# Storing each tile of gathered embeddings in three parts, and loading its first unit in another order

## The reference: what is computed

```
e = stack([tbl_f[ids[:, f]] for f in range(24)], axis=1)      # 1024 x 24 x 16
Xk = X0 = e
for W in (W0, W1, W2):                                        # 64 outputs each
    Xk = einsum('bfd,bhd,fho->bod', X0, Xk, W)                # products of every field with every row of Xk
    outs.append(Xk.sum(axis=2))
h = concatenate(outs + [dense_ctx], axis=1)                   # 1024 x 208
y = relu(relu(h @ W_top1 + b1) @ W_top2 + b2) @ W_top3        # 1024 x 1
```

## Time and profile before

| what | value |
|---|---|
| median of three runs | 424.27 us (423.68 to 428.24) |
| profiled execution, its own time | 421.92 us |
| its span, from first to last instruction | 420.1 us |
| mean granted TensorE clock | 0.955 |
| TensorE busy | 342.1 us, 81% |
| VectorE busy | 288.5 us, 69% |
| ScalarE busy | 189.7 us, 45% |
| POOL busy | 233.2 us, 55% |
| DMA, moved | 73.63 MB, mean 175 GB/s |

### The profile page before, as it was taken

One profiled execution on the slowest core, in us unless ns is written; L12 is line 12 of the kernel. 1 busy time (PEld: TensorE's weight loads), 2 busy tenths in 40 slices (PEclk: granted clock), 3 DMA queues, 4 the chain that ended last, 5 costly groups with the idle time before them and its releaser, 6 DMA issues.

```text
span 420.1 us, 6106 instructions
## 1 busy us (share of the span) xinstructions
PE 342.1 (81%) x2296; PEld 150.5 (36%) x2296; DVE 288.5 (69%) x277; ACT 189.7 (45%) x346; POOL 233.2 (55%) x252
## 2 busy tenths in 40 slices
PE   0045899438396969599999997999999999999997
PEld 0043422102041323244333433543444344443466
DVE  2001499129385959578987998798899999898700
ACT  1000026113335345273737573757556475745374
POOL 5775888888888888788788887677400000000000
PEclk9998899859886999999999999999999999999999
DMA  3355936499799998999799979998999799731000
GB/s 101 74 111 116 231 83 157 83 231 234 164 242 233 252 257 152 228 231 213 163 228 223 232 137 222 233 235 163 225 251 266 156 251 258 214 107 44 2 2 2
DMA packets 59263, 73.63 MB, mean 175 GB/s; under 512 B 31489, under 2 KB 36609, under 8 KB 59234
## 3 DMA queue, kind: packets, MB, share of 16 engines
q1 hardware_dynamic: 53090, 71.66, 74.2%
q0 software_dynamic: 6144, 1.59, 3.2%
HBM read 48.05 MB, written 1.58 MB: 118 GB/s over the span
## 4 chain that ended last, share of the span: by engine, by line
PE 68%; DMA 10%; issue 9%; POOL 3%; another core or an unknown queue 2%; ACT 2%; SPq 2%; DVE 1%; DVEq 0%; ACTq 0%
PE ps_x L370 44%; PE ps_tower L370 9%; PE ps_turn L370 6%; PE ps_b L370 5%; POOL x_rows L191 3%; DMA A<-x_scratch 3%; DMA B_sb<-x_sb 2%; DMA x_scratch<-x_rows 2%; PE ps_turn L415 2%; PE ps_turn L423 1%; SPq L256 1%; DMA C<-x_scratch 1%; DVE Z L337 1%; PE ps_tower L376 1%
## 5 line engine op out<-in xcount | busy, mean ns | idle before, releaser
L347 DVE TENSOR_TENSOR Z<-A,ps_b 128x1024 f32<-128x1024 f32 x192 | 222.0, 1214 | 29.5 <-remote 18.8
L191 POOL DMA_INDIRECT x_rows<-tbl,ids_sb x192 | 190.8, 994 | 62.6 <-issue 43.6
L370 PE MATMUL ps_x<-Z,w_sb 128*64 128x512 f32 x768 | 188.4, 609 | 1.7 <-issue 1.0
L337 DVE TENSOR_TENSOR Z<-A,C 128x1024 f32<-128x1024 f32 x48 | 58.1, 1224 | 75.5 <-DMA C<-x_scratch 37.4
L370 PEld LDWEIGHTS ps_x<-Z,w_sb 128*64 128x64 f32 x768 | 50.3, 139 | 84.3 <-issue 65.8
L370 PE MATMUL ps_x<-Z,w0s_sb 128*64 128x512 f32 x192 | 48.3, 626 | 24.4 <-DVE Z L337 23.9
L635 ACT ACTIVATE x_diag<-ps_turn,mask_sb 128x192 f32<-128x192 f32 x128 | 50.6, 606 | 9.9 <-PE ps_turn L423 9.8
L618 ACT COPY ps_b<-B_sb 128x1024 f32<-128x1024 f32 x45 | 46.4, 1030 | 9.8 <-DMA B_sb<-x_sb 5.9
L648 ACT COPY G<-ps_turn 128x416 f32<-128x416 f32 x31 | 15.7, 506 | 73.5 <-remote 45.8
L599 ACT COPY x_sb<-ps_x 128x512 f32<-128x512 f32 x16 | 9.4, 586 | 78.2 <-PE ps_x L370 78.2
L204 POOL MEMSET pause_sb<- 128x768 f32 x56 | 42.3, 756 | 3.6 <-DMA x_scratch<-x_rows 3.6
(11 more groups left out here) (48 smaller groups left out, 147.2 us busy)
## 6 DMA issues: line engine op xcount, KB each, us to landing
A<-x_scratch SPq DMA_DIRECT2D x48, 512.0 KB
B_sb<-x_sb SPq DMA_DIRECT2D x90, 256.0 KB
C<-x_scratch SPq DMA_DIRECT2D x32, 512.0 KB
x_rows<-tbl,ids_sb POOLq DMA_INDIRECT x192
x_quarters<-x_scratch SPq DMA_DIRECT2D x16, 96.0 KB
x_scratch<-x_rows SPq DMA_DIRECT2D x7, 192.0 KB
w_sb<-w SPq DMA_DIRECT2D x2, 384.0 KB
C<-x_scratch SPq DMA_DIRECT2D x2, 256.0 KB
```

Source lines behind the costliest of these rows:

```text
L191: pool.indirect_dma_start(out=x0_rows[t % 2][:, f * D:(f + 1) * D], out_offset=None, in_=tables[f], in_offset=bass.IndirectOffsetOnAxis(ap ...
L337: nc.vector.tensor_tensor(Z[s % ZR][:, :], A[u % AS][i][:, :], C[u % 2][i][:, :], ALU.mult).then_inc(z_ready, 1)
L347: nc.vector.tensor_tensor(Z[s % ZR][:, :], A[u % AS][i][:, :], ps_b[j % 2][:, :], ALU.mult)\
L370: return nc.tensor.matmul(out, lhsT, rhs, start=start, stop=stop)
```

## The change

The store of every tile is cut into the three parts that tile 0 has. Part i waits for its own 8 gathers and has its own semaphore. SP issues parts 0 and 1 where it stored the whole tile. For the first (even) unit of a tile it then loads `A 0` (needs part 0), `C 0` and `A 1` (need parts 0 and 1), issues the store of part 2, waits for it, and loads `C 1` and `A 2`. For odd units the order becomes `C 0`, `A 0`, `C 1`, `A 1`, `A 2`. For tile 1, part 0 is stored ahead of the `B` loads of unit 1, and part 1 behind them. POOL waits for each part of the tile before last ahead of that part's gathers, in place of one wait for the whole.

```diff
-            def store_tile(t):
-                sp.wait_ge(gathered[t % 2], 16 * F * ((t + 1) // 2))
-                store_rows(t, slice(0, F), x0_stored[t % 2])
+            def store_part(t, i):
+                sp.wait_ge(part_gathered[t % 2][i], 16 * FR * (t // 2 + 1))
+                v = x0_dram[t:t + 1, FR * i:FR * (i + 1), :].rearrange("t f (b d) -> (t b) f d", d=D)
+                src = x0_rows[t % 2][:, D * FR * i:D * FR * (i + 1)].rearrange("p (f d) -> p f d", d=D)
+                sp.dma_start(v, src).then_inc(part_stored[t % 2][i], 16)
...
                 for f in range(F):
+                    if t >= 2 and f % FR == 0:
+                        wait_stored(pool, t - 2, f // FR)
...
                 if u == 2:
+                    store_part(1, 0)
                     for k in range(NJ - 1):
                         load_b(u - 1, k)
-                    store_tile(1)
-                if u % 2 == 0:
-                    wait_stored(sp, u // 2)
+                    store_part(1, 1)
                 sp.wait_ge(z_ready, made_x1(u - 2, NI - 1))
-                for i in range(NI - 1):
-                    load_c(u, i)
                 for i in range(NI):
+                    if u % 2 == 0 and i > 0:
+                        wait_stored(sp, u // 2, i)
+                    if u % 2 == 0 and i == 1:
+                        load_c(u, 0)
+                    if u % 2 == 0 and i == 2:
+                        load_c(u, 1)
+                    if u % 2 == 1 and i < NI - 1:
+                        load_c(u, i)
+                    if u % 2 == 0 and i == 0:
+                        wait_stored(sp, u // 2, 0)
                     if u >= AS:
                         sp.wait_ge(z_ready, made_x2(u - AS, NP2 - NI + i))
                     load_a(u, i)
+                    if u % 2 == 0 and i == 1:
+                        store_part(u // 2, 2)
...
                 if u % 2 == 1 and u + 1 < UNITS:
-                    store_tile((u + 1) // 2)
+                    for i in range(NI - 1):
+                        store_part((u + 1) // 2, i)
```

More of the change, by code:

```diff
@@ L128, in cin_tower @@
         ids_in = sem("ids_in")
[L129 to L132, removed]
+        part_gathered = [[sem(f"part_gathered{p}{i}") for i in range(NI)] for p in range(2)]
+        part_stored = [[sem(f"part_stored{p}{i}") for i in range(NI)] for p in range(2)]
         ident_in, mask_in, pick_in, w0_in, w1_in, tower_in = (sem(n) for n in (
@@ L175, in after, with wait_stored @@
                 engine.wait_ge(semaphore, count)
[L177 to L182, removed]
+        def wait_stored(engine, t, i):
+            engine.wait_ge(part_stored[t % 2][i], 16 * (t // 2 + 1))
         block = ctx.enter_context(nc.Block())
@@ L196, in _ @@
             for f in range(F):
-                gather(0, f, gathered_part[f // FR])
-            pool.wait_ge(part_stored[NI - 1], 16)
+                gather(0, f, part_gathered[0][f // FR])
+            wait_stored(pool, 0, NI - 1)
             for t in range(1, TILES):
-                if t >= 2:
-                    wait_stored(pool, t - 2)
                 for f in range(F):
+                    if t >= 2 and f % FR == 0:
+                        wait_stored(pool, t - 2, f // FR)
                     if f % BURST == 0:
@@ L207, in _ @@
                     after(pool, z_ready, PER_SLOT * (2 * t - 5) + 2 * PER_SLOT * f // F)
-                    gather(t, f, gathered[t % 2])
+                    gather(t, f, part_gathered[t % 2][f // FR])
         @block.sync
@@ L264, in _ @@
             for i in range(NI):
-                sp.wait_ge(gathered_part[i], 16 * FR)
-                store_rows(0, slice(FR * i, FR * (i + 1)), part_stored[i])
-                sp.wait_ge(part_stored[i], 16)
+                store_part(0, i)
+                wait_stored(sp, 0, i)
                 if i > 0:
@@ L560, in _ @@
             pe.wait_ge(ident_in, 16)
-            pe.wait_ge(part_stored[1], 16)
+            wait_stored(pe, 0, 1)
             keep_warm(WARM[0])
```

## The result

| | before | the change |
|---|---|---|
| median of 20 runs | 423.77 us (419.96 to 428.24) | 424.02 us (421.86 to 432.55) |
| ratio, 95% interval | 1 | 1.0073 (1.0039 to 1.0107) |
| profiled execution, its own time | 421.92 us | 425.59 us |
| its span | 420.1 us | 423.7 us |
| granted TensorE clock, mean | 0.955 | 0.944 |

The ratio leaves disturbed executions out, so it says more than the two medians. The change costs 0.7%, some 3 us, where a gain of 2.7 us was predicted. The two spans differ by 3.6 us.

A forecast was written before the change was run, and what follows sets the result against it. TensorE (busy 81% of the span) and a nearly full DMA queue were taken as bounds. A 6.7 us opening gain less five extra pauses of 0.8 us gave -2.7 us from 424.27: 421.5 us predicted, range 416.5 to 429.

The forecast's parts named there:

- d = 0.8: Later tiles: two DMA queue pauses per tile last 0.8 us longer together than today's one of 2.6 us.
- The pause behind part 2: Later tiles, before `C 1`: SP waits for part 2's store, queue dry some 2.0 us, at most 3.0.
- the pause before `A 0`: Later tiles: SP waits for part 0, partly filled by part 1's store and the quarters, leaving 0.9 to 1.9 us.
- the lower bound: Later tiles: both pauses sum to 2.9 us, an extra of 0.3 us per tile over today's one.
- the skewed rings: Later tiles' DMA queue: rings skewed by full loads lengthen a pause, so the extra was put above its smallest value; no separate size.
- The upper bound, 2.3: Later tiles: both pauses as long as today's, 4.9 us together, an extra of 2.3 us per tile.
- the sum it gave, +3.3: Whole kernel: a fixed 2.0 us per additional waited store in each tile gives -6.7 + 10, slower by 3.3 us.
- the opening's term: Unit 2: three loads moved into the nearly idle queue bring its `B` 6.7 us earlier; 6.5 us for the engines.
- part 2's store is issued at 75.1: Tile 1: SP issues this store when it issued the whole one, but behind `A 1`; it lands at about 80.4 us.
- -6.7 + 5d: TensorE's shift at unit 14: the opening's 6.7 us gain less five tiles' extra pauses, predicted -2.7 us.
- The rival of the double pause: Even units: the queue drains twice at full price, 2.3 us extra per tile, time 429.1 us; chance 0.2.
- My slack: ScalarE's copy of `C`: room before a later `C 1` delays it, 9.0 us at unit 6, 3.0 at 12, 1.2 at 14.

The follow-up runs named there:

- the opening alone: Against the kernel before, only tile 1 is stored in three parts with the new load order for unit 2; tiles 2 to 7 stay whole, old order: ratio 1.0038.

## Why the prediction was wrong

**The step that failed: d = 0.8, the extra pause of a later tile.** It is 2.2 to 2.3 us by the dry stretches (1.6 by the count over all of them) and 2.3 on average by the copies of slots 5 to 15. The pause behind part 2 was put at 2.0 to 3.0 us and is 2.5. What was mis-sized most is the other one: the pause before `A 0` was put at 0.9 to 1.9 us, because part 1's store and the quarters would fill it, and it is 2.4. They fill next to nothing. I chose d near the lower bound because the part stores are small. The size of the store hardly matters: the queue is dry for 2.4 and 2.5 us with stores of a third, for 2.6 with whole ones. No trace takes a pause apart into receipt, issue and first byte, and no run shows the skewed rings that the choice of d mentions. The upper bound, 2.3, is what was measured. The rule of the Trainium skill that was weighed (page "DMA: Bandwidth & Descriptors", section "Anatomy of one DMA — SWDGE (gpsimd) path", a fixed cost of about 2.0 us) was nearer than my choice; that section speaks of DMAs issued by GpSimd, while these stores are issued by SyncE, and the 2.2 to 2.3 us of the trace agree with it in size. That the sum it gave, +3.3, is close to the +3.6 of the spans is chance, since the opening's term was off.

**The opening: the mechanism held, its size was off.** The loads started about when predicted (`A 0` issued at 69.61, DMA share 0.92). The step that part 2's store is issued at 75.1 "as the whole store was" failed by 5.4 us, since the last gathers land 5.2 us after the end of POOL's instruction when the queue is full, not 1.3. Unit 2's `B` came 3.4 us earlier and not 6.7 (4.4 on the later chip). That the change then was 8.1 ahead in slot 5 of the first chip is not its merit by these steps.

**POOL was in the way at unit 4.** Part 2 of tile 2 was stored at 119.76, predicted about 120, but that agreement is luck. SP had issued `A 1` at 114.41 and then stood for 4.8 us, until the last gather of tile 2, which POOL had ended at 113.20, had landed:

```profile
114.41 0.60 SPq L226 DMA_DIRECT2D A<-x_scratch  x1
119.76 0.38 SPq L219 DMA_DIRECT2D x_scratch<-x_rows  x1
```

`C 1` was issued at 125.52, and ScalarE waited 9.6 us for it. A part of the lead went past tile 2's gathers (3.8 us in slot 4); with a wait for the whole tile POOL takes nearly all of it away.

**The sum.** The form -6.7 + 5d was sound as far as the trace tells. With what was measured in slot 5 and d = 2.3 it is -8.1 + 11.5 = +3.4, where the spans differ by 3.6. With d = 2.3 and the predicted opening it would have been +4.8, as the rival of the double pause said, and with the 3.4 us of unit 2's `B` +8.1. The rival of the double pause had d right. That the loss stayed at 3 to 4 us rests on the first chip's slot 5, which is luck.

**The slack at ScalarE's copy of `C`.** I expected tile 3 to pay nothing and unit 14 to wait. On the first chip it was the other way: units 6, 8 and 10 waited 9.7, 6.4 and 5.0 us. My slack took queue and engines to be early by the same amount. But at unit 6 the queue was 2.7 ahead (158.62 against 161.31), the engines 8.1 in slot 5, and at unit 10 `C 1` landed 7.5 later in its unit instead of 5.4. On the later chip every even unit waited, unit 6 for 8.9 us and also unit 14, for 7.6. So tile 3 pays on both chips, against the prediction, and the wait in unit 14 came on one of them.

**The clock was left out.** The prediction counts waits alone. In the later tiles the granted clock fell three times where the kernel before held 1.00, and what that adds was not measured by itself.

**Smaller edits:** the two more DMAs a tile and POOL's waits cost nothing that shows. Three small stores in place of a large one were taken as neutral apart from d, and gain 1.2% where nothing stands between them, for a reason that stays open.

## What to carry to other kernels

Before a store is put behind loads and waited for, look for what keeps the queue busy meanwhile: here nothing was queued behind it, and each such wait left the queue dry for some 2.5 us, although the store was small. (A kernel with other work behind the store was not run.) Splitting a store paid when all its parts were issued ahead of the loads (0.988), and cost when one was put behind them (1.017 and 1.036). A pause can cost more than its dry time, where TensorE stands still for it and its clock falls. A lead that one stage wins is kept only up to the next wait for a producer with its own pace, so speed that producer (here POOL) in the same edit.

## What the runs showed of the hardware that was not expected

- **Gathers issued by POOL land late when the load queue is full:** 1.3 and 1.4 us after the instruction's end with little else in flight, 3.4 to 5.5 us in six traces with 512 KB loads in flight (4.4 with the opening alone, 5.2 in the change), and 6.6 us at tile 2 of the change (ended 113.20, stored 119.76).
- **Store and load of a part:** from the issue of part 2's store behind three loads to the issue of the load that needs it, 8.0 to 8.3 us in all five later tiles.
- **The same kernel differs from one measurement to another by more than the change:** 424 us for the kernel before at first, 413 to 414 on the two chips of the experiments, with 45.8 us of nameless ScalarE waits at `G` in the first trace (22.2 in the change's) and none in the later ones. Whether the chip or something else on it makes the difference isn't shown.
- **A stall of TensorE is followed by a lower clock:** after 3.80 us of standing still the granted clock was 0.57 from 266 to 270 us, and eight products took 3.24 us instead of 1.89.
